# A correlation stage whose batches are summed turned, with its inputs loaded during attention

## What is computed

```
q  = (layernorm(x) @ Wq + bq).transpose(0, 2, 1)      # Wq: 256 x 16
k_ = (ctx @ Wq + bq).transpose(0, 2, 1)               # v is the same as k_
corr = real(ifft(fft(q) * conj(fft(k_)))).mean(axis=(0, 1))   # 512 lags, over batches and heads
W_topk, I_topk = top_k(corr, 12); W_topk = softmax(W_topk)
R3 = sum over (w, shift) of w * roll(v, -shift)
x = x + R @ Wout + bout        # R: R3 repeated for 16 heads, reshaped as (B, 16*16, L) -> (B, L, 256)
```

## Time and profile before

| | us |
|---|---|
| three runs of the kernel | 2709.25, 2717.05, 2712.6 (median 2712.6) |
| profiled execution, its own time | 2706.32 |
| its span, first to last instruction | 2704.3 |
| TensorE busy in the span | 2299.8 (85%), mean granted clock 0.921 |
| VectorE, ScalarE, GpSimd busy | 1270.6, 848.1, 866.2 |

### The profile page before, as it was taken

One profiled execution on the slowest core, in us unless ns is written; L12 is line 12 of the kernel. 1 busy time (PEld: TensorE's weight loads), 2 busy tenths in 40 slices (PEclk: granted clock), 3 DMA queues, 4 the chain that ended last, 5 costly groups with the idle time before them and its releaser, 6 DMA issues. The chain is left out here.

```text
span 2704.3 us, 39994 instructions
## 1 busy us (share of the span) xinstructions
PE 2299.8 (85%) x12186; PEld 1627.9 (60%) x12187; DVE 1270.6 (47%) x2717; ACT 848.1 (31%) x1915; POOL 866.2 (32%) x1109
## 2 busy tenths in 40 slices
PE   6998856673999926698888887999999999999998
PEld 3454834442777722243333333655589999999998
DVE  5554135344444446677677765379322222222222
ACT  2222202220444403455565565322212222222221
POOL 2000003563000043654344121122235444445544
PEclk9999656886999967899899999999999999999999
DMA  9993116222555543544334220410047777777775
GB/s 338 372 365 133 58 28 249 86 95 81 157 156 156 152 125 83 106 111 101 71 73 102 67 72 13 162 39 16 16 139 245 246 245 245 246 249 247 247 246 168
DMA packets 246074, 412.60 MB, mean 153 GB/s; under 512 B 29958, under 2 KB 223855, under 8 KB 237784
## 3 DMA queue, kind: packets, MB, share of 16 engines
q1 hardware_dynamic: 206040, 351.70, 38.4%
q0 software_dynamic: 39936, 59.70, 10.7%
HBM read 261.83 MB, written 148.89 MB: 152 GB/s over the span
## 5 line engine op out<-in xcount | busy, mean ns | idle before, releaser
L2544 PE MATMUL me_hp<-me_xgT,me_w 128*128 128x160 f32 x3072 | 440.2, 300 | 0.6 <-DVE me_xgT L2586 0.6
L2544 PEld LDWEIGHTS me_hp<-me_xgT,me_w 128*128 128x128 f32 x3072 | 424.6, 191 | 1.5 <-DVE me_xgT L2586 0.7
L1349 DVE TENSOR_REDUCE hd_nmax<-hd_wide 128x2 f32<-128x1024 f32 x256 | 307.7, 1219 | 128.5 <-PE hd_wide L1094 124.3
L1278 ACT ACTIVATE hd_prob<-hd_slim 128x512 f32<-128x512 f32 x512 | 276.2, 601 | 190.4 <-PE hd_slim L1105 157.6
L2600 DVE TENSOR_TENSOR me_hid<-me_act_out,me_hp 128x160 f32<-128x160 f32 x384 | 123.5, 322 | 371.8 <-ACT me_act_out L2572 354.2
L1105 PE MATMUL hd_slim<-hd_q_stack,hd_k_stack 100*128 100x512 bf16 x512 | 199.9, 394 | 43.1 <-ACT hd_prob L1278 32.8
L2553 PE MATMUL me_op<-me_hid,me_w 128*128 128x160 f32 x1536 | 235.9, 303 | 0.0
L1094 PE MATMUL hd_wide<-hd_k_stack,hd_q_stack 97*128 97x512 bf16 x512 | 201.3, 398 | 29.5 <-DVE hd_rest L1343 15.9
L2572 ACT ACTIVATE me_act_out<-me_hp 128x160 f32<-128x160 f32 x384 | 116.8, 304 | 346.0 <-PE me_hp L2544 346.0
L2553 PEld LDWEIGHTS me_op<-me_hid,me_w 128*128 128x128 f32 x1536 | 213.7, 190 | 2.6
L1105 PEld LDWEIGHTS hd_slim<-hd_q_stack,hd_k_stack 100*128 100x128 bf16 x512 | 50.2, 99 | 197.7 <-ACT hd_prob L1278 84.7
(11 more groups left out here) (384 smaller groups left out, 3731.2 us busy)
## 6 DMA issues: line engine op xcount, KB each, us to landing
me_w<-in_L_ffn_w_exp SPq DMA_DIRECT2D x64, 2304.0 KB
places<-z_zero SPq DMA_DIRECT2D x64, 1152.0 KB, 11.2
mr_e_xt<-places SPq DMA_DIRECT2D x160, 144.0 KB, 2.2
outputs<-mr_e_y SPq DMA_DIRECT2D x160, 128.0 KB, 1.7
part_rows<-hd_parts SPq DMA_DIRECT2D x48, 256.0 KB
hd_k_stack<-part_rows SPq DMA_DIRECT2D x192, 64.0 KB
hd_q_stack<-part_rows SPq DMA_DIRECT2D x192, 64.0 KB
mr_w<-in_L_ffn_w_in SPq DMA_DIRECT2D x4, 2048.0 KB
```

What stands on the lines that cost most here:

```text
L1278: nc.scalar.activation(prob[:, u, :], slim[:, slim_slot(bt, item), :], ACT.Exp, scale=D ** -0.5)\
L1349: nc.vector.tensor_reduce(nmax[:, g % 2, n // 2, c:c + 2], wide[:, at], AX.X, ALU.max, negate=True)\
L2544: last = nc.tensor.matmul(hp[:, f % 3, half * CAP:(half + 1) * CAP], w1[:, sl, c, cols], xgT[:, sl, c, :], start=(c == 0), stop=(c == DC - 1))
```

## The change

It rewrites the front of `mix_correlation`, and with it small parts of the middle and the back.

- The context has four slots. A new class `CorrelationInputs` holds them and the weights; its `load`, put into `meanwhile` ahead of the stores of zero rows, loads the weights and the first four batches of context during attention. Batches 4 to 7 are loaded when the turning of the batch four before is evicted.
- `wq` comes from the host with 112 zero columns on either side. A slice of 128 columns of it, the 16 of weights at the place of batch b among zeros, is now the stationary operand, and the turned tokens, 512 columns, move. All eight batches add up in one PSUM buffer of queries and one of keys (`acc`), which so are already turned: row 16 b + d. `q_tok`, the turning of both and their copies go; `k_tok` is made from `kT` by four transposes and one eviction by ScalarE.
- TensorE turns the next context before it projects the context of the batch before, and likewise for x. `xn` has four slots, so that VectorE norms ahead.
- `h` and the weights are held once, and the DMA reads them two or three times over.
- In the back the products go to four buffers (`tp`), one addition covers the four tiles of a batch, and the batches 2, 4 and 6 are evicted by ScalarE to `y` and added by GpSimd.

Where a run of removed lines is long, "..." stands for it; they are lines 468 to 618 of the listing above.

```diff
--- before.py
+++ after.py
...
+class CorrelationInputs:
...
+        self.cx = k.sb("cx", [P, self.SLOTS, TB, D])
+        self.wq = k.sb("wq", [P, DC, (2 * B - 1) * self.DH])
+        self.bq = k.sb("bq", [P, 1])
+        self.wo = k.sb("wo", [P, DC, D])
...
+    def load_ctx(self, sp, b):
+        sp.dma_start(self.cx[:, b % self.SLOTS], self.ctx_tok[b]).then_inc(self.ctx_loaded[b % self.SLOTS], 16)
+    def load(self, sp):
+        w_q, b_q, w_out, b_out = self.sources
+        sp.dma_start(self.wq[:], w_q.rearrange("(c p) n -> p c n", p=P)).then_inc(self.loaded, 16)
+        sp.dma_start(self.bq[:], b_q[:, :]).then_inc(self.loaded, 16)
+        sp.dma_start(self.wo[:], w_out.rearrange("(c p) n -> p c n", p=P)).then_inc(self.loaded, 16)
+        sp.dma_start(self.bo[:], b_out.rearrange("(a n) -> a n", a=1)).then_inc(self.loaded, 16)
+        for b in range(self.SLOTS):
+            self.load_ctx(sp, b)
...
-        xn = k.sb("xn", [P, 2, TB, D])
-        cx = k.sb("cx", [P, 2, TB, D])
+        xn = k.sb("xn", [P, SLOTS, TB, D])
...
+        USES = [(what, b, c) for b in range(B) for what in ("ctx", "x") for c in range(DC)]
+        BY_POOL = (2, 4, 6)
...
+                for b in range(SLOTS, B):
+                    sp.wait_ge(tp_free, uses_through("ctx", b - SLOTS))
+                    given.load_ctx(sp, b)
+                sp.wait_ge(h_out, 1)
+                sp.dma_start(h_dram.rearrange("p (a n) -> p a n", a=2), h[:].unsqueeze(1).to_broadcast([P, 2, S])).then_inc(h_stored, 16)
                 sp.wait_ge(h_stored, 16)
...
+                sp.dma_start(h_skew[:], bass.AP(tensor=h_dram.tensor, offset=0, ap=[[2 * S + 1, P], [1, S]])).then_inc(h_back, 16)
+                sp.wait_ge(c_ready, 1)
+                sp.dma_start(c_dram.rearrange("a (n m) -> a n m", n=3), weight[:].unsqueeze(1).to_broadcast([1, 3, S])).then_inc(c_stored, 16)
...
+                for n, b in enumerate(BY_POOL):
+                    pool.wait_ge(y_out, n + 1)
+                    xs = x[:, b * TB:(b + 1) * TB, :]
+                    nc.gpsimd.tensor_tensor(xs, xs, y[:, n % 2, :].unsqueeze(1).to_broadcast([P, TB, D]), ALU.add).then_inc(x_done, 1)
...
-                with pe.Fori(0, TURNS) as i:
-                    for sl in range(2):
-                        b = i * 2 + sl
+                def turn(what, b):
+                    if what == "x":
                         pe.wait_ge(xn_ready, b * TB + TB)
...
+                    else:
+                        pe.wait_ge(given.ctx_loaded[b % SLOTS], 16 * (b // SLOTS) + 16)
+                    for c in range(DC):
+                        use = USES.index((what, b, c))
+                        if use >= 4:
+                            pe.wait_ge(tp_free, use - 3)
+                        for j in range(TB):
+                            src = (xn if what == "x" else cx)[:, b % SLOTS, j, c * P:(c + 1) * P]
+                            last = nc.tensor.transpose(tp[:, use % 4, j * P:(j + 1) * P], src, ident[:])
+                        last.then_inc(tp_full, 1)
+                def project(what, b):
+                    pe.wait_ge(tp_free, uses_through(what, b))
+                    src, to = (xT, 0) if what == "x" else (cT, 1)
+                    for c in range(DC):
+                        last = nc.tensor.matmul(acc[:, to, :], wq[:, c, (B - 1 - b) * DH:(2 * B - 1 - b) * DH], src[:, b % 2, c, :],
+                                                start=(b == 0 and c == 0), stop=(b == B - 1 and c == DC - 1))
+                    if b == B - 1:
+                        last.then_inc(acc_full, 1)
+                turn("ctx", 0)
+                turn("x", 0)
+                pe.wait_ge(given.loaded, 64)
+                for b in range(1, B):
+                    turn("ctx", b)
+                    project("ctx", b - 1)
+                    turn("x", b)
+                    project("x", b - 1)
+                project("ctx", B - 1)
+                project("x", B - 1)
+                pe.wait_ge(acc_out, 2)
                 for j in range(TB):
+                    if j:
+                        pe.wait_ge(acc_out, 3)
                     last = nc.tensor.matmul(misc[:, 0, :], kT[:, j * P:(j + 1) * P], qT[:, j * P:j * P + S],
                                             start=(j == 0), stop=(j == TB - 1))
                 last.then_inc(h_full, 1)
+                for j in range(TB):
+                    last = nc.tensor.transpose(misc[:, 1, j * P:(j + 1) * P], kT[:, j * P:(j + 1) * P], ident[:])
+                last.then_inc(k_turned, 1)
...
                 pe.wait_ge(z_ready, 2)
+                pe.wait_ge(tp_free, len(USES))
                 for b in range(B):
-                    if b >= 2:
-                        pe.wait_ge(y_free, b - 1)
-                    o = proj[:, b % 2, 0:D]
+                    if b >= 4:
+                        pe.wait_ge(y_free, len([n for n in range(b - 3) if n not in BY_POOL]))
+                        pe.wait_ge(y_out, len([n for n in range(b - 3) if n in BY_POOL]))
+                    o = tp[:, b % 4, 0:D]
...
+                norm_at = USES.index(("x", 0, 0))
+                for n, (what, b, c) in enumerate(USES):
+                    if n == norm_at:
+                        norm.scalar(act, 0)
+                    act.wait_ge(tp_full, n + 1)
+                    nc.scalar.activation((xT if what == "x" else cT)[:, b % 2, c, :], tp[:, n % 4, :], ACT.Copy).then_inc(tp_free, 1)
+                act.wait_ge(k_turned, 1)
+                nc.scalar.activation(k_tok[:].rearrange("p j n -> p (j n)"), misc[:, 1, :], ACT.Copy).then_inc(k_ready, 1)
                 act.wait_ge(ntop_ready, 1)
                 nc.scalar.activation(weight[:], corr[:, 0:S], ACT.Exp, bias=ntop[:]).then_inc(weight_ready, 1)
+                for n, b in enumerate(BY_POOL):
+                    act.wait_ge(y_full, b + 1)
+                    if n >= 2:
+                        act.wait_ge(x_done, n - 1)
+                    nc.scalar.activation(y[:, n % 2, :], tp[:, b % 4, 0:D], ACT.Copy).then_inc(y_out, 1)
...
+                for b in range(B):
+                    if b >= SLOTS:
+                        dve.wait_ge(tp_free, uses_through("x", b - SLOTS))
+                    for j in range(TB):
+                        t = b * TB + j
+                        nc.vector.tensor_scalar(xn[:, b % SLOTS, j, :], x[:, t, :], mean[:, t:t + 1], rstd[:, t:t + 1],
+                                                ALU.subtract, ALU.mult).then_inc(xn_ready, 1)
+                chain.link(nc.vector.memset(corr[:], PAD))
+                dve.wait_ge(given.loaded, 64)
+                dve.wait_ge(acc_full, 1)
+                nc.vector.tensor_scalar(kT[:], acc[:, 1, :], bq[:], None, ALU.add).then_inc(acc_out, 1)
+                dve.wait_ge(acc_full, 2)
+                for n in range(2):
+                    nc.vector.tensor_scalar(qT[:, n * S:(n + 1) * S], acc[:, 0, :], bq[:], None, ALU.add).then_inc(acc_out, 1)
                 dve.wait_ge(h_full, 1)
-                nc.vector.tensor_copy(h[:, 0:S], misc[:, 0, :]).then_inc(h_out, 1)
-                nc.vector.tensor_copy(h[:, S:2 * S], misc[:, 0, :]).then_inc(h_out, 1)
-                chain.link(nc.vector.memset(corr[:], PAD))
+                nc.vector.tensor_copy(h[:], misc[:, 0, :]).then_inc(h_out, 1)
...
-                for n in range(3):
-                    nc.vector.tensor_scalar(c3[:, n, :], weight[:], wr[:], None, ALU.mult).then_inc(c_ready, 1)
+                nc.vector.tensor_scalar(weight[:], weight[:], wr[:], None, ALU.mult).then_inc(c_ready, 1)
...
+                    xs = x[:, b * TB:(b + 1) * TB, :]
+                    if b in BY_POOL:
+                        dve.wait_ge(x_done, BY_POOL.index(b) + 1)
+                    else:
+                        dve.wait_ge(y_full, b + 1)
+                        nc.vector.tensor_tensor(xs, xs, tp[:, b % 4, 0:D].unsqueeze(1).to_broadcast([P, TB, D]), ALU.add).then_inc(y_free, 1)
+                        dve.wait_ge(y_free, len([n for n in range(b + 1) if n not in BY_POOL]))
...
+            def meanwhile(sp):
+                given.load(sp)
+                clear_rows(sp)
...
+    beside = (B - 1) * i["L0_xattn_Wq"].shape[1]
+    a["L0_xattn_Wq"] = np.pad(i["L0_xattn_Wq"], ((0, 0), (beside, beside)))
+    a["L0_xattn_bq"] = np.tile(i["L0_xattn_bq"], B).reshape(P, 1)
...
```

144 lines of the change are left out of this document (31 added, 113 removed).

## The result

| | before | after |
|---|---|---|
| median of 4 runs each, us | 2714.56 (2709.25 to 2717.05) | 2670.62 (2668.67 to 2677.38) |
| profiled execution, its own time | 2706.32 | 2668.67 |
| its span | 2704.3 | 2666.3 |
| mean granted clock | 0.921 | 0.931 |
| correlation stage, its first row to the first of the next stage | 265.44 to 420.26: 154.8 | 265.13 to 383.40: 118.3 |

After over before is 0.9848, 95% interval 0.9831 to 0.9865: faster by 44 us of the medians, by 37.65 between the profiled executions. The stage is 36.5 us shorter; about 1 us lies elsewhere.

What follows compares the result with a forecast made beforehand. TensorE was taken to bound the front through idle gaps, 16-column projections and a low clock. Terms -31.1 - 2.6 - 2.3 - 0.6 - 0.8 + 1.2 = -36.2 us gave 2670.1 profiled, median 2676; range 2671 to 2682, with rivals 2664 to 2697.

Steps and rivals of the forecast that it cites:

- Start: Head of the front: x of batch 0 turned at 271.7 us (sum 271.76), hardly before 272.2; only context 0's turning gained.
- Steady front: Turning and projecting after the start: 13.1 + 27.5 us plus 2.4 warm-up, ending at 314.9 against 346.0, -31.1 us.
- The 2.4 us gaps go: Front: TensorE's 2.4 us idle ahead of each later pair of batches disappears, as ScalarE and VectorE stay ahead.
- (a): Middle, last projection to lag product: one VectorE addition replaces eight transposes and three copies, 3.5 to 0.9 us, -2.6.
- (b): Middle, lag product: at the full clock level it takes 3.6 us instead of 5.9, -2.3.
- (c): Middle, lag product's end to the store: one copy of h instead of two, 1.36 us to 0.7 + 0.05, -0.6.
- (f): Middle, scalings: one of three stays, 1.27 to about 0.45 us, -0.8.
- (d): Middle, trip of h through DRAM: reading each row twice may change it by -0.3 to +1.5 us; taken as 0.
- Back: Eight last products: TensorE keeps 3.16 us a batch, while giving batches 2, 4 and 6 to GpSimd lengthens the tail, +1.2 us.
- Loads ahead: Weights and four context batches loaded during attention: cost nothing; up to 9 us if SyncE's barrier wait were gone.
- the first (half level throughout): Rival, front: clock stays at the half level throughout, making the kernel 5.3 us slower, median 2718; chance 6%.
- Rival 3: Back runs at the full clock level: some 21 us against 29, 8 us less, median 2668; chance 7%.

Runs made afterwards that it cites:

- the best version: Changed kernel with the root first on ScalarE, the bias added to x by GpSimd, and GpSimd adding batches 1, 3, 5, 6: median 2602.45 beside 2652.36, ratio 0.9814.

## Why the prediction held, point by point

The forecast for the profiled execution was 2670.1; it is 2668.67. For the median it was 2676, with 2671 to 2682 as its own range and 2664 to 2697 with the rivals; at 2670.6 the median lies just under the first and inside the second. Most of the terms held, one by one, and those that were off cancel in part: the front gave 1.0 us more than forecast and the back cost 0.4 less, the middle gave 0.8 less.

- **Start.** 271.25 against 271.76, and by the wait that was named: VectorE for the root, the root behind two evictions.
- **Steady front.** From there to the last product 42.65 us against 43.2; the warm-up took 2.05 (42.65 less 13.1 and 27.5) against 2.4 and 0.2. The step that carried the forecast, that wide products keep the clock up, holds: 1.00 from 280 to 310. The experiments show more than I had argued. The kernel before lost its clock to 16 columns, and neither to its pauses nor to the number of weight loads. To the end of the last projection, the new order with the loads ahead gives 0.3 us, 128 columns alone 17 (to the lag product 17.3), all together 31.8. The order shows its worth only with the wide products: with 16 columns it lowered the clock from 0.63 to 0.50 (280 to 340 us), which ate up the pauses saved.
- **Pauses.** "The 2.4 us gaps go" was right, but it doesn't take projections and turning in turn: in pairs, with the context turned first, 0.60 us of each is left, and the lag product is 2.5 us later in all.
- **Middle.** (a) -2.7 against -2.6; (b) 3.70 us against 3.6; (c) and (f) as said, 0.76 from the lag product's end to the store and 0.47 for the scaling. (d) was taken at 0 within -0.3 to +1.5: the trip of h is 5.74 (319.20 to 324.94) against 5.24, **+0.5**. "The weights' trip stays as it is" failed: 333.29 to 343.36 is 10.07, before 371.28 to 380.70, 9.42: **+0.65**. Both lie in the store, which now reads one copy two or three times. From the store to the load behind it, which waits for it, the queue before shows:

```profile
359.41 0.34 SPq L483 DMA_DIRECT2D xa_h_skew<-lag_products  x1
...
371.28 0.24 SPq L486 DMA_DIRECT2D lag_weights<-xa_c  x1
372.58 1.75 SPq L489 DMA_DIRECT2D xa_hankel<-lag_weights  x4
```

That is 2.61 us for h (356.80 to 359.41) and 1.30 for the weights; after it is 3.19 (319.20 to 322.39) and 2.02. The ten other traces part the same way: 2.70 and 1.29 in the old kernel with 128 columns, which still makes the copies, 3.15 to 3.20 and 2.02 to 2.03 in the nine that don't. The bytes are the same, but the trip of h has 416 packets in place of 288. So holding h and the weights once saves 1.4 us of copies and gives 1.3 back in the stores. The middle's -2.9 against a forecast -3.7 is these two, less 0.3 for the products behind them (6.45 against 6.77).
- **Back.** +0.8 against +1.2: the clock stayed at 0.50, as forecast, and the last statistics end 3.7 us behind product 7 instead of 4.1, because GpSimd's addition takes 2.34 (I took 2.6) and VectorE's 1.21 (1.3). That GpSimd's share lengthens the tail is shown too: without it the tail is 2.70.
- **Loads ahead.** Free, as said: attention moves 323 GB/s instead of 305 and is no longer. That they gain something I had put at context 0's turning; with them at the head of the stage the changed kernel's stage is 7.5 us longer.

Of the rivals, the first (half level throughout) did not come: the 16-column kernel is nearest to it, 60 us at 0.50 but warm at both ends, and its lag product still starts 3 us earlier than before. The rule of the Trainium skill, TensorE: Matmul & The Clock Gate, Part 4 (PE-mode transpose), by which the full rate does not engage for transposes, isn't borne out here by fp32 transposes: a third of the new front is transposes and eight of them take 1.04 us at clock 1.00, against 1.97 at 0.50. Rival 3 was set aside because the instructions are the same, and that holds for this change; but the reason missing there ("no row says why it is 0.50") has now been found in the one-row products. The rival put the full level at 8 us; without the one-row products the back is 10 us shorter.

**The step that was off** is the last, from the profiled execution to a median. I added to the forecast the 6.3 us by which the profiled execution of before lay under its median (8.2 with the fourth run); after, the profiled execution lies only 2.0 under its own. Which of its runs a kernel is profiled in is chance, and the forecast took it for a constant. So the median came out at 2670.6 instead of 2676, with a term by term sum that was right to 1.5 us.

**Still open:** how much the whole kernel gains. The stage shortens by 36.3 to 36.5 us in both traces of the changed kernel, but medians fell by 44 on the first chip (37 to 46 within the interval of the ratio) and by 31 on the other (24 to 34). Of the other kernels with several runs, three agree to 0.6 us, whole and stage: 20.1 and 19.9 with 128 columns, 4.8 and 5.3 with 16 columns, 49.9 and 49.4 for the best version; in pairs it is 33.8 and 36.8. Of the five with one run, one agrees (39.2 and 38.7 without GpSimd), and four gain 5 to 11 us less in the whole than in the stage (18.3 and 29.0 with the loads late). What follows the stage varies by 7 us among the ten traces, 2228 to 2235 us, which is as much as most of these gaps; no run shows what sets it. The kernel before was not traced on the other chips, so its stage there is taken to be as long as on the first.

## What to carry to other kernels

Read the granted clock next to the busy share: TensorE was 100% busy at 0.50 here because of the shape of its products, and padding 16 columns to 128 with zeros (17 us) or taking a one-row bias product out (10 us) was worth more than a reordering at that level (0.3 us). Look at clock first and order second: a better order gained little here until the clock was up. A copy saved on an engine can come back in the DMA that then reads its source several times, so set the two against each other. And give an engine that idles through the stage (GpSimd here) the small addition that would otherwise go through TensorE.

## What of the hardware was unexpected

- TensorE busy without a break at clock 0.50 for 60 us with 16-column fp32 products and transposes in turn; the same order with 128 columns in as many records 1.00.
- A batch of four records of 256 columns and two of a one-row product: 3.16 us at 0.50 for all eight batches. Without the one-row product the clock rises within 4 us and a batch takes 0.85.
- Transposes of 128x128 fp32 alone bring the clock up (before, from 272.2 to about 275.5 us) and hold it among wide products. Across a pause of 2.4 us the full level was kept at three places of three (1.09 us for eight behind it), and lost 1.5 us later at one of them.
- GpSimd's additions of 128x1024 fp32 take 2.3 us each, with VectorE idle (18.54 for eight) or at work (9.27 for four). VectorE's statistics take 1.41 us with GpSimd's share in the back and without it.
- A store of 128x512 fp32 that writes each row twice lands 2.6 us after its issue from two copies in SBUF and 3.2 us from one copy read twice.
- The same kernel takes 2714 us on one chip and 2652 on others, while the correlation stage of the changed kernel is as long to 0.2 us on both; what follows the stage takes 2283 us on the first and 2228 on the other.
